# Expert layer: the last four experts' weights requested one at a time as tiles finish, and the last tile's second product by row halves

## The reference

```
logits = x_flat @ Wg + bg
assignments = argmax(softmax(logits))
h   = gelu(x_flat @ W1[e] + b1[e])          # e: the one expert of a token, of 8
out = x + w * (h @ W2[e] + b2[e])           # w: the probability of that expert
```

## Time and profile before

| | |
|---|---|
| runs of the kernel | 1970.99, 1971.99, 1972.17 us, median 1971.99 |
| span of the profiled execution, first to last instruction | 1969.3 us |
| PE busy over the span | 1878.3 us (95%) |
| DVE, ACT, POOL busy | 69%, 57%, 50% |
| first tile's turning on PE to last scatter issued | 1658.85 to 1961.33 us of the span |

### The profile page before, as it was taken

The page is one execution under the profiler, slowest core; times in us unless marked ns, Lnnn a source line. Parts: engine busy times, 40 slices in busy tenths (PEclk is TensorE's granted clock), DMA queues, the critical chain, the costliest instruction groups (busy, mean ns, idle before and its releaser), DMA issues. The chain is left out here.

```text
span 1969.3 us, 34918 instructions
## 1 busy us (share of the span) xinstructions
PE 1878.3 (95%) x10950; PEld 1325.4 (67%) x10950; DVE 1349.2 (69%) x2849; ACT 1128.1 (57%) x2168; POOL 975.0 (50%) x1144
## 2 busy tenths in 40 slices
PE   6999999999999999999999999999999875899997
PEld 4667777777777766666666666666666454798896
DVE  5667667676766676667676757576665476788886
ACT  3555555555555555555565656565555444688885
POOL 3455456445555555455454445554454442355454
PEclk9999999999999999999999999999999886999999
DMA  6455554645555573644444545535353456722220
GB/s 186 120 142 126 131 133 97 148 108 119 116 138 132 130 187 88 140 109 110 102 112 108 129 108 123 114 91 125 87 113 81 103 191 197 266 67 93 84 89 17
DMA packets 137658, 239.18 MB, mean 121 GB/s; under 512 B 31066, under 2 KB 32386, under 8 KB 137440
## 3 DMA queue, kind: packets, MB, share of 16 engines
q1 hardware_dynamic: 108704, 190.49, 35.5%
q0 software_dynamic: 21392, 45.37, 11.6%
q10 hardware_dynamic: 7408, 1.42, 0.4%
HBM read 114.84 MB, written 48.97 MB: 83 GB/s over the span
## 5 line engine op out<-in xcount | busy, mean ns | idle before, releaser
L558 ACT ACTIVATE attn_probs<-attn_sT 128x512 f32<-128x512 f32 (+3 forms) x1024 | 528.6, 518 | 475.8 <-PE attn_sT L872 472.8
L466 POOL TENSOR_TENSOR attn_probs<-attn_probs 128x512 f32<-128x512 f32 (+2 forms) x384 | 531.2, 1402 | 179.1 <-PE attn_o_ps L887 130.4
L667 DVE TENSOR_REDUCE attn_m_col<-attn_sS 128x1 f32<-128x512 f32 x512 | 342.7, 688 | 194.2 <-PE attn_sS L856 186.5
L872 PE MATMUL attn_sT<-attn_stack 98*128 98x512 f32 (+2 forms) x1024 | 387.1, 389 | 0.3 <-ACT attn_probs L558 0.3
L856 PE MATMUL attn_sS<-attn_stack 97*128 97x512 f32 (+2 forms) x1024 | 369.2, 371 | 14.4 <-DVE attn_m_col L667 3.3
L673 DVE CUSTOM_DVE_ANT_0 attn_sS<-attn_sS,attn_cT_low 128x128 f32<-128x128 f32 x496 | 241.1, 504 | 171.0 <-PE attn_sS L856 167.4
L872 PEld LDWEIGHTS attn_sT<-attn_stack 98*128 98x128 f32 x1024 | 188.2, 189 | 206.0 <-ACT attn_probs L558 127.8
L454 POOL TENSOR_SCALAR_AFFINE_SELECT attn_probs<-attn_probs 128x256 f32<-128x256 f32 x256 | 119.6, 467 | 345.2 <-ACT attn_probs L558 345.1
L856 PEld LDWEIGHTS attn_sS<-attn_stack 97*128 97x128 f32 x1024 | 193.5, 190 | 70.9 <-DVE attn_m_col L667 15.5
L887 PE MATMUL attn_o_ps<-attn_probs,attn_V 128*32 128x512 f32 (+3 forms) x2048 | 233.6, 527 | 5.0 <-ACT attn_probs L558 2.0
L836 PE MATMUL attn_pj<-attn_xT_high,attn_w_high 128*128 128x512 f32 x384 | 153.8, 400 | 1.4 <-DVE attn_xT_low L651 1.4
(11 more groups left out here) (212 smaller groups left out, 3703.8 us busy)
## 6 DMA issues: line engine op xcount, KB each, us to landing
attn_stack<-attn_stage SPq DMA_DIRECT2D x666, 128.0 KB, 2.3
attn_rows<-in_x_dram SPq DMA_DIRECT2D x64, 256.0 KB, 4.1
attn_rows<-x_after_self SPq DMA_DIRECT2D x64, 256.0 KB, 4.1
moe_w<-in_L_ffn_W_dram SPq DMA_DIRECT2D x16, 1024.0 KB, 15.2
attn_stack<-attn_stage POOLq DMA_DIRECT2D x96, 128.0 KB, 3.3
x_after_self<-attn_rows SPq DMA_DIRECT2D x32, 256.0 KB, 2.6
x_after_self<-in_L_attn_b_dense_dram POOLq DMA_DIRECT2D x32, 256.0 KB, 4.9
attn_rows<-in_ctx_dram SPq DMA_DIRECT2D x32, 256.0 KB, 3.0
```

What stands on the lines that cost most here:

```text
L466: pool.tensor_tensor(total, total, tile_of(n, kb)[:, js, q0:S], ALU.add).then_inc(added, 1)
L558: act.activation(tile_of(n, kb)[:, j, q0:S], sT[:, i % 2, q0:S], ACT.Exp, scale=SCALE).then_inc(exp_done, 1)
L667: dve.tensor_reduce(to, sS[:, k % 2], AX_X, ALU.max).then_inc(s_free, 1)
L872: pe.matmul(sT[:, i % 2, q0:S], stack[0:ROW_MAX + 1, n % 2, 1, j, kb * P:(kb + 1) * P], stack[0:ROW_MAX + 1, n % 2, 0, j, q0:S], start=Tru ...
```

## The change

SP's part: after the first three `b2` rows only experts 2 and 3 are requested at once. Each of experts 4 to 7 is requested right behind the `b2` row of tile 3, 4, 5 and 6, and that row waits for the residual of tile 0, 1, 2 and 3 (`resid_ready`). The `b2` rows of tiles 7 and 8 follow, and SP's loop begins at tile 9 in place of tile 3. PE's part: in the last tile only, the second product runs with r outside and k inside.

```diff
@@ -961,6 +961,7 @@
     FIRST_LAPS = -(-E // RING)
+    PACED_LAPS = 1 + -(-(E - NB) // RING)
@@ -1132,11 +1133,15 @@
             for i in range(RING):
                 tile(0, i)
             sp.wait_ge(placed, 4)
-            for e in range(SOON, E):
-                if e < NB:
-                    sp.wait_ge(loaded[weight_sem[e]], 16)
+            for e in range(SOON, NB):
+                sp.wait_ge(loaded[weight_sem[e]], 16)
                 load_weights(e)
-            with sp.Fori(1, LAPS) as lap:
+            for e in range(NB, E):
+                tile(1 + (e - NB) // RING, (e - NB) % RING)
+                load_weights(e)
+            for i in range((E - NB) % RING, RING):
+                tile(PACED_LAPS - 1, i)
+            with sp.Fori(PACED_LAPS, LAPS) as lap:
                 for i in range(RING):
                     tile(lap, i)
@@ -1630,16 +1635,18 @@
                 pe.wait_ge(y_taken, R * t + R)
-                for k in range(KT):
-                    if k % KC == 0:
-                        pe.wait_ge(w2_low, CH * t + (k // KC + 1))
-                    pe.wait_ge(h_low, KT * t + (k + 1))
-                    for r in range(R):
-                        for n, (x, y) in enumerate(SPLIT):
-                            op = pe.matmul(py[:, r], hT[x][:, k, r * P:(r + 1) * P], w2[y][:, k],
-                                           start=k == 0 and n == 0, stop=k == KT - 1 and n == len(SPLIT) - 1)
-                        if k == KT - 1:
-                            op.then_inc(y_full, 1)
+                by_rows = [(k, r) for r in range(R) for k in range(KT)]
+                by_depth = [(k, r) for k in range(KT) for r in range(R)]
+                for k, r in by_rows if last else by_depth:
+                    if r == 0:
+                        if k % KC == 0:
+                            pe.wait_ge(w2_low, CH * t + (k // KC + 1))
+                        pe.wait_ge(h_low, KT * t + (k + 1))
+                    for n, (x, y) in enumerate(SPLIT):
+                        op = pe.matmul(py[:, r], hT[x][:, k, r * P:(r + 1) * P], w2[y][:, k],
+                                       start=k == 0 and n == 0, stop=k == KT - 1 and n == len(SPLIT) - 1)
+                    if k == KT - 1:
+                        op.then_inc(y_full, 1)
```

## The result

The changed kernel takes 1979.01 us (median of 5 runs, 1977.52 to 1980.32) against 1971.99 (5 runs, 1970.31 to 1972.95): ratio 1.0039, 95% interval 1.0026 to 1.0051. It is 7.0 us slower, where I had forecast 5 us faster, with a chance of 0.10 for slower. The profiled execution took 1980.32 us.

A forecast was written before the change was run, and what follows sets the result against it. PE bounds the layer at 12.24 us a tile, plus an 8.48 us DMA stall at tile 3. Saving 4.5 there and 0.55 in the last tile takes the span from 1969.3 to 1964.2, median 1966.9; range 1962.8 to 1971.6.

The forecast's parts named there:

- What bounds the kernel: Expert layer: PE at 12.24 us a tile, plus one 8.48 us stall at tile 3 from the DMA load.
- When SP asks, and the size of the burst: SP's queue: 4 MB burst over before 1678 us, then four pairs at about 1679, 1692, 1704 and 1717 us.
- The 2.36 MB run from 1680.7 for 6.0 us at 390 GB/s: Beside tile 0's scatter: a `b2` row and weight pair start 1.5 to 2 us after request, then stream at full rate.
- I take c = 1.0: Tiles 0 to 3: the weights add 1.0 us between handing over rows and the normalize three tiles later.
- There is hardly any load when the gather follows (from 1690 on): Tile 3's second gather: the paced weights are over by then, so only the scatter ahead of it is delayed.
- the prediction's own formula: Tile 0's cost over the floor: usual path 14.25 us plus the weights' added lateness, less 15.0 us free.
- its allowance: Tile 0, handing over to normalize three tiles later: 15.0 us are free before PE loses time.
- the sum: Tiles 0 to 3: 0.25 us for tile 0 and 1.25 for each other, 4.0 in place of 8.48.
- The fair share by the Trainium skill: Scatters beside weights: half of 390 GB/s, 0.5 MB in 2.6 us in place of 1.3, so 1.3 us added.
- A wait of a microsecond does not lower the clock: PE's short waits: tile 7's wait left its turning at 1.04 us, so the old stall's clock loss is saved too.
- The last tile: PE's row halves let the last scatter start about 1.8 us behind the last matmul, not 2.3: 0.55 us saved.
- four stalls for one, slower: POOL's wait ahead of L1218: scatters of tiles 0 to 3 each land after 6.1 us; 1975.8 us, chance 0.08.

The follow-up runs named there:

- The smaller pieces: Full change, experts 4 to 7 requested in 256 KB pieces, two or four outstanding: 1968.93 us (two), 1967.62 us (four).
- the kernel with W1 only: The change's weights part without the last tile's part, requesting only W1 of experts 4 to 7, W2 left out: 1973.05 us.
- no late weights: The kernel before the change, with experts 4 to 7 never requested nor waited for: 1964.93 us, ratio 0.996.
- the kernel with one expert held back: Against before: row halves, experts 2 and 4 early, 3, 5, 6 in the burst, 7 later in 256 KB pieces, four outstanding: 1967.41 us.
- two early experts: Against before: row halves, experts 2 and 4 requested ahead of the gate, 3, 5, 6, 7 in the burst: 1968.85 us, ratio 0.9977.
- with three: Against before: row halves, experts 2, 4 and 5 requested ahead of the gate, 3, 6, 7 in the burst: 1968.64 us, ratio 0.9982.

## Why the prediction was wrong, point by point

**What bounds the kernel: right, with one reading wrong.** The stall came of DMA load beside tile 0's scatter and gather, and was worth 8.5 us in the trace. Without the late requests it is gone, and the time falls by 7 us. But I put the whole of the gather's 7.96 us against 3.55 down to the load. Its issue took 3.37 us against 1.01, so 2.4 of the 4.4 us are POOL's issue beside DVE's four splits, and only 2.0 lie behind it.

**When SP asks, and the size of the burst: right.** Pairs at 1679.9, 1693.2, 1714.3 and 1726.2 us; the last two are later than the 1704 and 1717 forecast because the stalls push the tiles back.

**"The 2.36 MB run from 1680.7 for 6.0 us at 390 GB/s": wrong in its start.** They take 10 us from the request, where I had 7.7. The median landing of a 1 MB request among these eight is 9.6 us. Full rate begins at 1684 and then lasts somewhat under 6 us. I gave the `b2` row its bytes (256 KB in 0.65 us) and not its own pace, 100 to 120 GB/s at a busy share of 0.8 to 0.9. The kernel with the `b2` row behind the pair confirms it, full rate after 2 us.

**"I take c = 1.0": this step failed.** Of the scatter alone the lateness was 6.70 - 3.01 = 3.7 us in tile 0, 3.4 in tile 1, 4.7 in tile 2, 3.4 in tile 3, that is at or over the 3.2 of the burst, which I had taken for the price of a load with no end in sight. (Against the 3.48 and 2.64 us of its own tiles 2 and 3 without load it is 4.2 and 3.8.) A finite pair costs as much. The smaller pieces show it from the other side: 1.2 us with two outstanding, 1.8 with four, in tile 0. So what SP has outstanding beside the indirect DMA counts, and not how long the load will last. It need not have been asked for ahead of it, as tile 2's gather shows in the kernel with W1 only.

**"There is hardly any load when the gather follows (from 1690 on)": this failed with it, and it is the greater part.** With no late weights the second gather would be issued at 5.5 us behind the second scatter, and be over at 9.0. With a scatter 3.7 us late it is issued at 1693.15, the next pair at 1693.19, and it is late by another 8.60 - 3.52 = 5.1 us. Of these, 3.37 - 1.02 = 2.35 are the issue, which now falls beside DVE's four splits, and 2.7 lie behind it, beside the pair. From the second scatter's issue to the normalize there are 1701.77 - 1683.52 = 18.25 us in place of 9.0: c = 9.2 for tile 0, where I had 1.0. Put into the prediction's own formula it gives 14.25 + 9.2 - 15.0 = 8.5 us, and the trace has (19.22 - 12.24) + (14.04 - 12.24) = 8.8, but that they agree is partly luck. The formula has no term for the clock, to which I put the 1.8 us of the second period, and its allowance is too small: from the handing over at 1678.51 to the normalize at 1701.77 there are 23.26 us, and tile 3 came 6.98 late, so 16.3 us were free and not 15.0. The rows of before say the same, 22.56 - 6.25 = 16.3. Tile 2 repeats it, 4.7 on the scatter and 4.8 on the gather (2.0 of them the issue, 2.97 us), and costs 6.9 + 2.3 = 9.1. Tiles 1 and 3 cost nothing, though the sum charged each of the four tiles alike: I put it down to PE's stall just before them, which gives their chain some 7 us of slack. So of four pairs every second one made a stall, two in all, 17.9 us over the floor where I had 4.0 and before had 8.5.

**The fair share by the Trainium skill** (page "DMA: Bandwidth & Descriptors", section "Queues, rings and completion order": an engine takes a packet from each of its queues in turn). By it I had worked out c = 1.3. The trace does not agree with that working: 3.4 to 4.7 us on the scatters. (The page counts packets; that both queues' packets are alike, which "half" needs, was my assumption.) Whether the indirect DMA starts late behind what is queued or is served slowly all the way, the runs here don't tell apart.

**"A wait of a microsecond does not lower the clock": it stood on one row, of tile 7, and doesn't bear on this result.** The waits of the change were 6.6 to 6.8 us, and the granted clock fell to 0.50 in each. The period after each stall, 14.0 and 14.5 us, holds 1.8 and 2.3 us of it. In the kernel with one expert held back, PE's wait ahead of tile 4 was only 1.58 us, 0.7 us more of idle time followed, and then the clock was at 0.50 for 3.4 us. At half the clock these cost 1.7 us (an estimate), which with the 0.7 makes up most of the 2.8 that the next period took over the floor.

**The last tile: right.** The same rows as the earlier trace rows in the changed kernel:

```profile
1965.14 0.75 DVE L1541 SCALAR_TENSOR_TENSOR moe_rows<-moe_py,moe_rows 128x512 f32<-128x512 f32 x1 [0.44 <-PE moe_py L1646]
...
1966.77 0.98 POOL L1240 DMA_INDIRECT out_dram<-moe_rows,moe_cur  x1 [1.85 <-DVE moe_rows L1541]
...
1967.44 0.40 PE L1646 MATMUL moe_py<-moe_w_high,moe_hT_low 128*128 128x512 f32 x1
1967.95 0.75 DVE L1541 SCALAR_TENSOR_TENSOR moe_rows<-moe_py,moe_rows 128x512 f32<-128x512 f32 x1 [2.06 <-PE moe_py L1646]
1969.58 0.98 POOL L1240 DMA_INDIRECT out_dram<-moe_rows,moe_cur  x1 [1.83 <-DVE moe_rows L1541]
```

The last scatter starts 1969.58 - 1967.84 = 1.74 us after the last matmul's end, against 1960.35 - 1958.02 = 2.33: saved 0.59, forecast 0.55. PE's 24 matmuls show no gap. The run with this part alone agrees (its ratio can't tell 0.6 us from nothing); the two kernels with the weights part differ by 1982.76 to 1979.01, more than 0.6. In their profiled executions (4.3 us apart) 3.5 us of that lie ahead of the expert layer, which the change doesn't touch: SP's first load of the gate stands at 1604.07 and 1600.61. From there to PE's last turning they took 349.01 and 348.79 us.

**The rivals.** Nearest was "four stalls for one, slower", with its place (POOL's wait for the scatter) and its price (3.2 us or more). Its time, 1975.8, was still low, as it didn't have the gather's part. I gave it 0.08 because "2.36 MB are gone in 6 us"; at full rate they nearly are, but a load of that length cost a scatter as much as the burst.

## What to carry to other kernels

A transfer that is spread over the program by hanging it on a step of a pipeline meets the same neighbour every time; before spreading, ask of each later stage what its own small DMA will meet once the first has made it late. Here the one burst stalled one tile of 23; a paced pair made a scatter late, and through that lateness the gather met both the next pair and DVE's splits. What helped was to have little outstanding beside the small DMA (requests of 256 KB, two to four outstanding), or to move requests ahead of the place where anything waits for small DMAs; neither got more than about 0.2% (4 us) of the 0.4% that were there.

## What the runs showed of the hardware that was not expected

- An indirect scatter of 128 rows beside 2 MB of SP's requests lands in 6.4 to 7.7 us in the changed kernel, in place of 2.6 to 3.5. In the burst of before it was no more, 6.3 us. With 0.5 MB outstanding it was 3.0 to 5.6. A gather beside them lands 5.2 us behind the end of its issue row, in place of 2.5 (8.60 - 3.37 against 3.52 - 1.02).
- An issue of an indirect DMA that began 0.3 to 0.7 us into DVE's run of four splits of 128x512 (2.49 us) nearly always ended 0.9 us or more behind that run, and took 2.7 to 4.1 us, with and without DMA load; of those that began with it, some took 1.0 to 1.5 us and the gather of the change's first stall 3.37. No run removed the splits, so that they are the cause is read from the rows alone.
- The 256 KB `b2` row, spread from one row over 128 partitions, holds the DMA engines at a share of 0.8 to 0.9 while 110 GB/s move, and delays the full rate of what stands behind it by 2 to 3 us.
- Writes of 16 KB on ACT's queue are late beside the same load too: 3.6 us to landing without load beside them, 10.6 with two early experts, 14.0 with three (medians of four).
